# Sums of exponentials in three cross attentions: added and spread by one product with ones, inverted on all partitions in quarters

## The chip, the cores and the metric

The kernel runs on one core of one Trainium2 chip. TensorE does matrix products into eight PSUM banks of 128 x 512 float32; VectorE, ScalarE and GpSimd work on SBUF, the first two on PSUM as well; SyncE issues the loads. Each engine works through its own list of instructions in order, and they meet at semaphores. The metric is the device time of one execution in microseconds.

## The reference

Twelve sublayers of a small Perceiver: four rounds of cross attention, self attention and a feed-forward part over x, 8 sequences of 64 tokens of width 256. Three of the four cross attentions (L0, L1 and L3) read the 1601 rows of the context with 16 heads of 128. L1 and L3 have a mask (here all ones) and L0 normalises queries and keys by their root mean square. What matters here, from L3:

```python
scores = jnp.einsum('bhtd,bhsd->bhts', q, k) / scale
mask = vision_mask[:, None, None, :]
scores = jnp.where(mask, scores, -jnp.inf)
attn = jax.nn.softmax(scores, axis=-1)
attn = jnp.nan_to_num(attn, nan=0.0)
out = jnp.einsum('bhts,bhsd->bhtd', attn, v)
```

A softmax over 1601 keys needs the maximum and the sum of the exponentials of every query, and divides the output by that sum. The fourth cross attention (L2, the kind "dca") goes through the same function by branches of its own.

## The kernel before

`context_columns` (L301) does scores, softmax and values of one cross attention. Keys lie on the partitions, in 13 tiles of 128 (the last has 65 rows); the 512 columns are 8 heads x 64 queries of one sequence. A group g is one such half of a sequence's heads, so there are 16 groups of 13 tiles, and a step i is one tile. All engines walk the same list of steps; what one does at a step for an earlier tile is written as a delay.

- TensorE, at each step: the score product of tile i (L466) into one of three banks, then the value product of tile i - 18 (L483, `VAL` = 18), accumulated over a group. A score product waits until the maximum of the tile three steps back is taken (`maxed`; in the rms kind until it is kept).
- ScalarE: the exponential of tile i - 17 in place (L585), then the copy of the scores of tile i to SBUF (`probs`, a ring of 20 tiles; L604). In the rms kind the keys' scale is applied on the way, on ScalarE (L600) for four tiles of 13 and on VectorE (L677) for the others.
- VectorE: the subtraction of the maxima from tile i - 16 (the shift, L666), then the running maximum of tile i over the partitions' own rows (L689; L687 or L691 for the first tile, L693 in the kinds without mask).
- GpSimd: the sum of the exponentials, tile after tile, into `acc` (L763 copies the first, L766 adds the others).
- In the rms kind also two products of the key projection per step (L420), their squares (L539, ScalarE) and sums of squares (L620, VectorE); in every second group a mean square (L641), a root (L589) and its inverse (L646 to L650) on the way to the keys' scale.

Over the partitions, sums and maxima are taken through TensorE. For the maxima: four turns of `top` (L498) into bank 4 (`T_BANK`) at step 0 of the next group, a reduction along the columns (L711), and four products that spread the result over all partitions (L507). For the sums of group g the same path runs at steps counted in the later group whose tile i is then at hand:

- step 5: TensorE turns `acc` in four pieces of 128 x 128 (L517) into bank 4;
- step 6: VectorE reduces to 128 x 4 (L716), in the masked kind clamps at 1e-30 (L719), and inverts (L729 in L0, L1 and L3);
- step 7: TensorE spreads the four columns by four products with the identity (L528) into bank 4; a float32 product is two instructions, a turn is one;
- step 8: VectorE multiplies the kept values in `QT` by bank 4 (L741). ScalarE had copied them there at step 5 (L578).

The turn of the maxima, L498, comes right behind the value product of step 0. It waits until VectorE has taken the maximum of the group's last tile (tile 12), and until the multiplication two groups back has read bank 4. After the last score step only the pipeline's end runs, and then `heads_out` (L771) begins with L786.

Of the kernel before, what the change touches and what calls it, by code (L numbers as in the profile page):

```python
# [300 lines left out]
def context_columns(nc, M, A, kind, scale, W):  # L301
# [13 lines left out]
    T_BANK, X_BANK = 4, 6  # L315
    HALF = 2 * BANK
# [4 lines left out]
    with ExitStack() as ctx:  # L321
# [5 lines left out]
        if not dca:  # L327
            rows = sb("ctx_rows", [P, 2, NT, CDIM])
# [12 lines left out]
        with stage(nc, "first_in", "keys_in0", "keys_in1", "keys_in2", "rows_in0", "rows_in1", "ready", "scored", "by_act",  # L341
                   "by_dve", "maxed", "top_turned", "most_ready", "most_spread", "shifted", "exped", "valued", "summed",
                   "value_kept", "sum_turned", "sum_ready", "sum_clamped", "rest_ready", "rest_spread", "divided", "folded",
# [67 lines left out]
            def _(pe):  # L411
# [38 lines left out]
                for i in STEPS:  # L450
# [61 lines left out]
                    if g is not None:  # L512
                        pe.wait_ge(S["summed"], NT * (g + 1))
                        if g + 1 < NG:
                            pe.wait_ge(S["most_ready"], g + 2)
                        for b in range(4):
                            last = nc.tensor.transpose(M.bank[T_BANK][:, b * P:(b + 1) * P], acc[:, g % 2, b * P:(b + 1) * P],  # L517
                                                       M.ident[:, :])
                        last.then_inc(S["sum_turned"], 1)
                    g = due(i, NT + VAL + 2)  # L520
                    if g is not None:
                        pe.wait_ge(S["rest_ready"], g + 1)
                        for b in range(4):
                            if dca:
                                last = nc.tensor.matmul(M.bank[T_BANK][32 * b:32 * b + 32, 0:P], apart[:, g % 2, b, :],
                                                        M.ident[:, :], start=True, stop=True)
# [88 lines left out]
            def _(dve):  # L615
# [43 lines left out]
                for i in STEPS:  # L659
# [53 lines left out]
                    if g is not None:  # L713
                        z = rest[:, g % 2, :]
                        dve.wait_ge(S["sum_turned"], g + 1)
                        nc.vector.tensor_reduce(z, turned, AX.X, ALU.add).then_inc(S["sum_ready"], 1)  # L716
                        if kind == "mask":
                            dve.wait_ge(S["sum_ready"], g + 1)
                            nc.vector.tensor_scalar(z, z, 1e-30, None, ALU.max).then_inc(S["sum_clamped"], 1)  # L719
                            dve.wait_ge(S["sum_clamped"], g + 1)  # L720
                        else:
                            dve.wait_ge(S["sum_ready"], g + 1)
                        if dca:
                            step(nc.vector.reciprocal(z, z))
                            nc.vector.tensor_tensor(apart[:, g % 2, :, :], z.unsqueeze(2).broadcast_to([P, 4, 32]),
                                                    pair[:, :].unsqueeze(1).broadcast_to([P, 4, 32]),
                                                    ALU.mult).then_inc(S["rest_ready"], 1)
                        else:
                            nc.vector.reciprocal(z, z).then_inc(S["rest_ready"], 1)  # L729
                    g = due(i, NT + VAL + 3)  # L730
                    if g is not None:
                        dve.wait_ge(S["rest_spread"], g + 1)
                        dve.wait_ge(S["value_kept"], g + 1)
                        if dca:
                            x, o = part[:, g % 2, :], M.OT[:, g % U, g // U * SEQ:(g // U + 1) * SEQ]
                            step(nc.vector.tensor_tensor(x, x, M.bank[T_BANK][:, 0:P], ALU.mult))
                            step(nc.vector.tensor_tensor(o, o, x[:, 0:SEQ], ALU.add))
                            nc.vector.tensor_tensor(o, o, x[:, SEQ:P], ALU.add).then_inc(S["divided"], 1)
                        else:
                            x = M.QT[:, g // U, HG * (g % U):HG * (g % U + 1), :]  # L740
                            nc.vector.tensor_tensor(x, x, M.bank[T_BANK].rearrange("p (h q) -> p h q", h=HG),  # L741
                                                    ALU.mult).then_inc(S["divided"], 1)

            @block.gpsimd
            def _(pool):
# [8 lines left out]
                for i in STEPS:  # L754
                    if 0 <= i - VAL < NI:
# [1742 lines left out]
```

## Time and profile before

| | us |
|---|---|
| median of 3 runs | 3653.46 |
| lowest and highest | 3650.73, 3654.89 |
| profiled execution: its time | 3651.31 |
| profiled execution: span from first to last instruction | 3649.6 |
| TensorE busy | 3019.9 |
| VectorE busy | 2369.7 |
| ScalarE busy | 1677.3 |
| GpSimd busy | 1147.3 |

The profile is one execution taken by the hardware profiler. Its time has 1.7 us around the span. A row in order of time begins with the start in us from the span's start and the length; what stands in brackets at its end is how long the engine was idle before and what ended that. Several like instructions in a row are merged, with their count (x8); neighbours on an engine can overlap by a little, so the spacing of starts is the cost of an instruction in a full queue, and the length is what a waiting one sees. PE is TensorE, PEld its weight load, DVE VectorE, ACT ScalarE, POOL GpSimd. L0's groups run from about 200 to 915 us, L1's from 1350 to 1770, L3's from 2950 to 3370.

### The profile page before, as it was taken

The page shows a single profiled execution, that of the slowest core. Times are in us where ns is not written, and L with a number is a line of the kernel's source. Part 1 is how long each engine was busy: PE and PEld are TensorE (multiplying, and loading weights), DVE is VectorE, ACT ScalarE, POOL GpSimd, SP SyncE. Part 2 cuts the span into 40 slices and gives each one's busy share as a digit, 9 for nine tenths or more (in the row PEclk, how much of TensorE's full clock was granted, in tenths as well). Part 3 has the DMA queues.
Part 4 walks back from the last instruction along what each step waited for, and adds up shares of the span by engine and source line. Part 5 has one row for each costly group of instructions (what it writes and reads, how often), then busy time and mean ns, then how long its engine had stood idle before and what let it go on. Part 6 is the DMA issues. An engine that isn't in the chain of part 4 may idle for free. (4 is left out here: it accounts for less than half of the span.)

```text
span 3649.6 us, 35780 instructions
## 1 busy us (share of the span) xinstructions
PE 3019.9 (83%) x10841; PEld 1534.1 (42%) x10842; DVE 2369.7 (65%) x3813; ACT 1677.3 (46%) x3342; POOL 1147.3 (31%) x952
## 2 busy tenths in 40 slices
PE   7899999998898979999813378888845789999896
PEld 2344444443566634444501233333324434444563
DVE  4688888887275437777295557777854357776246
ACT  2455555555242226666311156666611146665241
POOL 0023333336000006666260035565710036666000
PEclk9999999999899989999856689999957899999998
DMA  1100000000420020110010100000010121100301
GB/s 61 75 0 19 19 19 19 19 10 0 111 71 1 0 95 28 37 37 10 13 51 8 37 18 10 19 10 1 1 37 6 41 75 37 37 28 1 107 1 41
DMA packets 73488, 110.58 MB, mean 30 GB/s; under 512 B 15792, under 2 KB 61776, under 8 KB 71888
## 3 DMA queue, kind: packets, MB, share of 16 engines
q1 hardware_dynamic: 73296, 108.29, 9.2%
q8 instruction: 88, 1.44, 0.2%
q14 instruction: 104, 0.85, 0.1%
HBM read 107.23 MB, written 1.05 MB: 30 GB/s over the span
## 5 line engine op out<-in xcount | busy, mean ns | idle before, releaser
L766 POOL TENSOR_TENSOR acc<-acc,probs 128x512 f32<-128x512 f32 (+2 forms) x768 | 981.2, 1278 | 797.1 <-ACT probs L585 773.6
L466 PE MATMUL psum<-QT,ctxT 128*128 128x512 f32 (+1 forms) x1248 | 638.2, 597 | 29.2 <-DMA ctxT<-in_ctx_T 26.6
L483 PE MATMUL psum<-probs,ctx_rows 128*128 128x512 f32 (+1 forms) x1248 | 633.4, 594 | 17.0 <-ACT probs L585 7.3
L666 DVE TENSOR_TENSOR probs<-probs,psum 128x512 f32<-128x512 f32 (+2 forms) x832 | 558.4, 675 | 27.6 <-PE psum L507 27.6
L604 ACT COPY probs<-psum 128x512 f32<-128x512 f32 (+2 forms) x624 | 362.9, 582 | 286.1 <-PE psum L466 282.6
L420 PE MATMUL psum<-wk_sb,ctxT 128*128 128x512 f32 (+1 forms) x832 | 391.1, 598 | 28.8 <-DMA ctxT<-in_ctx_T 17.1
L689 DVE SCALAR_TENSOR_TENSOR top<-psum,hidden,top 128x512 f32<-128x512 f32 (+1 forms) x384 | 287.5, 749 | 155.2 <-ACT probs L604 153.1
L763 POOL COPY acc<-probs 128x512 f32<-128x512 f32 x64 | 45.4, 709 | 1056.5 <-ACT probs L585 1056.5
L483 PEld LDWEIGHTS psum<-probs,ctx_rows 128*128 128x128 f32 (+1 forms) x1248 | 234.0, 190 | 319.9 <-issue 278.6
L539 ACT ACTIVATE ksq<-psum 128x1024 f32<-128x1024 f32 (+1 forms) x208 | 212.5, 1022 | 314.5 <-PE psum L420 311.3
L466 PEld LDWEIGHTS psum<-QT,ctxT 128*128 128x128 f32 (+1 forms) x1248 | 218.9, 188 | 253.3 <-issue 207.4
L585 ACT ACTIVATE probs<-probs,hidden 128x512 f32<-128x512 f32 (+1 forms) x416 | 299.3, 724 | 56.0 <-DVE probs L666 55.8
L585 ACT ACTIVATE probs<-probs 128x512 f32<-128x512 f32 (+2 forms) x416 | 259.8, 627 | 62.0 <-DVE probs L666 61.3
L620 DVE TENSOR_REDUCE key_var<-ksq 128x8 f32<-128x1024 f32 (+1 forms) x208 | 251.7, 1211 | 34.3 <-ACT ksq L539 34.3
L420 PEld LDWEIGHTS psum<-wk_sb,ctxT 128*128 128x128 f32 (+1 forms) x832 | 153.5, 187 | 240.1 <-issue 182.4
L466 PE MATMUL psum<-QT,keysT 128*128 128x512 f32 (+1 forms) x416 | 229.0, 634 | 1.2 <-ACT keysT L563 1.2
L693 DVE TENSOR_TENSOR top<-probs,top 128x512 f32<-128x512 f32 x192 | 145.9, 760 | 108.9 <-ACT probs L600 104.4
L693 DVE TENSOR_TENSOR top<-psum,top 128x512 f32<-128x512 f32 x192 | 132.0, 688 | 101.7 <-ACT probs L604 101.2
L751 POOL TENSOR_TENSOR kn<-kn,rk 128x256 f32<-128x256 f32 (+1 forms) x104 | 62.6, 624 | 281.7 <-DVE rk L650 281.7
L434 PE MATMUL psum<-wkv,ctxT 128*128 128x512 f32 (+1 forms) x208 | 116.7, 650 | 10.8 <-DMA ctxT<-in_ctx_T 7.5
L600 ACT ACTIVATE probs<-psum,rk 128x64 f32<-128x64 f32 x512 | 111.3, 335 | 5.1 <-PE psum L466 5.1
L479 PEld LDWEIGHTS psum<-probs,vals 128*32 128x32 f32 (+1 forms) x1664 | 34.0, 111 | 178.2 <-ACT probs L585 79.5
(423 smaller groups left out, 4064.5 us busy)
## 6 DMA issues: line engine op xcount, KB each, us to landing
ctx_rows<-in_ctx_rows SPq DMA_DIRECT2D x24, 832.0 KB, 4.5
ctxT<-in_ctx_T SPq DMA_DIRECT2D x24, 800.5 KB, 5.4
ctxT<-in_ctx_T SPq DMA_DIRECT2D x8, 792.5 KB, 4.5
wq_sb<-in_L_xattn_Wq SPq DMA_DIRECT2D x3, 2048.0 KB, 7.8
wo_sb<-in_L_xattn_Wo SPq DMA_DIRECT2D x3, 2048.0 KB, 9.9
wd<-in_L_ffn_wd SPq DMA_DIRECT2D x1, 3072.0 KB, 11.5
w_q<-in_L_attn_w_aq SPq DMA_DIRECT2D x8, 256.0 KB, 3.3
w_o<-in_L_attn_w_ao SPq DMA_DIRECT2D x1, 2048.0 KB, 10.1
```

The lines of the kernel that those rows point to most:

```text
L420: last = nc.tensor.matmul(M.bank[bank + j][0:hi - lo, :], ctxT[:, s % KEYS, lo:hi], wk[:, half * HALF + j * BANK:half * HALF + (j + 1) * B ...
L434: nc.tensor.matmul(M.bank[X_BANK + t % 2][0:hi - lo, :], ctxT[:, s % KEYS, lo:hi], wkv[:, :], start=True, stop=True).then_inc(S["projected ...
L466: nc.tensor.matmul(M.bank[i % BANKS][0:m, :], key, M.QT[:, s, HG * (g % U):HG * (g % U + 1), :], start=True, stop=True).then_inc(S["scored ...
L483: last = nc.tensor.matmul(M.bank[V_BANKS[g % len(V_BANKS)]], rows[0:m, s % 2, t, :], probs[0:m, j % RING, :], start=t == 0, stop=t == NT - 1)
L539: nc.scalar.square(ksq[0:hi - lo, v % 2, :], flat[0:hi - lo, bank * BANK:bank * BANK + HALF]).then_inc(S["squared"], 1)
L585: nc.scalar.activation(x, x, ACT.Exp, bias=bias, scale=scale).then_inc(S["exped"], 1)
L604: nc.scalar.copy(probs[0:m, i % RING, :], M.bank[i % BANKS][0:m, :]).then_inc(S["by_act"], 1)
L620: nc.vector.tensor_reduce(var[0:hi - lo, s % SLOTS, t, HG * half:HG * (half + 1)], ksq[0:hi - lo, v % 2, :].rearrange("p (h d) -> p h d", ...
L666: nc.vector.tensor_tensor(x, x, M.bank[M_BANKS[g % len(M_BANKS)]][0:m, :], ALU.subtract).then_inc(S["shifted"], 1)
L689: last = nc.vector.scalar_tensor_tensor(x, bank, hidden[0:m, s, t:t + 1], x, ALU.add, ALU.max)
L693: last = nc.vector.tensor_tensor(x, kept if norm else bank, x, ALU.max)
L766: nc.gpsimd.tensor_tensor(a, a, x, ALU.add).then_inc(S["summed"], 1)
```

## The change

In the kinds "rms" and "mask" the path of the sums is replaced. At step 5 TensorE does one product of a 128 x 128 matrix of ones with `acc` (128 x 512) into bank 4, so that each partition holds the sum of every column. VectorE inverts bank 4 in four quarters of 128 columns into a new SBUF tensor `inverse`, one quarter at each of the steps 6 to 9, behind the maximum of the step. At step 10 it multiplies `QT` by `inverse`. The turns of `acc`, the reduction, the clamp, the small reciprocal and the four spreads are gone there; so that no sum is zero, GpSimd adds 1e-32 to the first tile of a group in the masked kind where it copied it. The turn of the maxima now waits for the four quarters of two groups back in place of the multiplication. The kind "dca" keeps its instructions; the branches are only written in another order. The core of the diff:

```diff
+    QUARTERS = 4
+            inverse = sb("inverse", [P, N])
...
                         if g >= 2:
-                            pe.wait_ge(S["divided"], g - 1)
+                            if dca:
+                                pe.wait_ge(S["divided"], g - 1)
+                            else:
+                                pe.wait_ge(S["inverted"], QUARTERS * (g - 1))
...
                         if g + 1 < NG:
                             pe.wait_ge(S["most_ready"], g + 2)
-                        for b in range(4):
-                            last = nc.tensor.transpose(M.bank[T_BANK][:, b * P:(b + 1) * P], acc[:, g % 2, b * P:(b + 1) * P],
-                                                       M.ident[:, :])
+                        if not dca:
+                            last = nc.tensor.matmul(M.bank[T_BANK], M.ones[:, :], acc[:, g % 2, :], start=True, stop=True)
...
                     g = due(i, NT + VAL + 2)
-                    if g is not None:
+                    if g is not None and dca:
...
-                            else:
-                                last = nc.tensor.matmul(M.bank[T_BANK][:, b * P:(b + 1) * P],
-                                                        rest[:, g % 2, b:b + 1].broadcast_to([P, P]), M.ident[:, :],
-                                                        start=True, stop=True)
...
-                        if kind == "mask":
-                            dve.wait_ge(S["sum_ready"], g + 1)
-                            nc.vector.tensor_scalar(z, z, 1e-30, None, ALU.max).then_inc(S["sum_clamped"], 1)
-                            dve.wait_ge(S["sum_clamped"], g + 1)
...
-                            nc.vector.reciprocal(z, z).then_inc(S["rest_ready"], 1)
+                    for n in range(QUARTERS):
+                        g = due(i, NT + VAL + 1 + n) if not dca else None
+                        if g is not None:
+                            dve.wait_ge(S["sum_turned"], g + 1)
+                            these = slice(n * N // QUARTERS, (n + 1) * N // QUARTERS)
+                            nc.vector.reciprocal(inverse[:, these], M.bank[T_BANK][:, these]).then_inc(S["inverted"], 1)
+                    g = due(i, NT + VAL + 1 + QUARTERS) if not dca else None
+                    if g is not None:
+                        dve.wait_ge(S["inverted"], QUARTERS * (g + 1))
+                        dve.wait_ge(S["value_kept"], g + 1)
+                        x = M.QT[:, g // U, HG * (g % U):HG * (g % U + 1), :]
+                        nc.vector.tensor_tensor(x, x, inverse[:, :].rearrange("p (h q) -> p h q", h=HG), ALU.mult).then_inc(S["divided"], 1)
...
-                            x = M.QT[:, g // U, HG * (g % U):HG * (g % U + 1), :]
-                            nc.vector.tensor_tensor(x, x, M.bank[T_BANK].rearrange("p (h q) -> p h q", h=HG),
-                                                    ALU.mult).then_inc(S["divided"], 1)
...
-                            nc.gpsimd.tensor_copy(a, x).then_inc(S["summed"], 1)
+                            if kind == "mask":
+                                nc.gpsimd.tensor_scalar(a, x, 1e-32, None, ALU.add).then_inc(S["summed"], 1)
+                            else:
+                                nc.gpsimd.tensor_copy(a, x).then_inc(S["summed"], 1)
```

## Rows read from the trace of the kernel before

**Rows 1.** Busy time by stretch: us, then PE, PEld, DVE, ACT, POOL, clock, DMA.

```profile
250.00:300.00 50.00, 49.27 (x133) 22.88 (x132) 41.91 (x55) 28.26 (x61) 16.34 (x13) 1.00 0.00 1
850.00:900.00 50.00, 45.07 (x138) 20.73 (x137) 41.54 (x68) 26.64 (x74) 35.86 (x27) 1.00 0.00 1
1500.00:1550.00 50.00, 49.39 (x151) 23.97 (x150) 38.52 (x62) 32.33 (x54) 30.89 (x26) 1.00 0.10 34
```

**Rows 2.** Order of time, TensorE, L1: start, length, engine, line, out<-in, idle before.

```profile
1512.33 0.60 PE L498 MATMUL psum<-ident,top 128*128 128x128 f32 x4
...
1520.53 1.02 PE L466 MATMUL psum<-QT,ctxT 128*128 128x512 f32 x2
...
1522.25 0.60 PE L517 MATMUL psum<-ident,acc 128*128 128x128 f32 x4
1522.68 1.02 PE L466 MATMUL psum<-QT,ctxT 128*128 128x512 f32 x2
...
1525.26 1.02 PE L483 MATMUL psum<-probs,ctx_rows 128*128 128x512 f32 x2
1526.59 1.16 PE L528 MATMUL psum<-ident,rest 128*128 128x128 f32 x8 [0.30 <-DVE rest L729]
1527.58 1.02 PE L466 MATMUL psum<-QT,ctxT 128*128 128x512 f32 x2
...
1537.88 0.60 PE L498 MATMUL psum<-ident,top 128*128 128x128 f32 x4
```

**Rows 3.** Order of time, VectorE, the same group of L1.

```profile
1524.36 0.75 DVE L689 SCALAR_TENSOR_TENSOR top<-psum,hidden,top 128x512 f32<-128x512 f32 x1 [0.57 <-ACT probs L604]
1525.03 0.68 DVE L716 TENSOR_REDUCE rest<-psum 128x4 f32<-128x512 f32 x1
1525.74 0.58 DVE L719 TENSOR_SCALAR rest<-rest 128x4 f32<-128x4 f32 x1
...
1526.45 0.66 DVE L666 TENSOR_TENSOR probs<-probs,psum 128x512 f32<-128x512 f32 x1
...
1530.52 0.68 DVE L666 TENSOR_TENSOR probs<-probs,psum 128x512 f32<-128x512 f32 x1
1531.12 0.74 DVE L689 SCALAR_TENSOR_TENSOR top<-psum,hidden,top 128x512 f32<-128x512 f32 x1
1531.78 0.68 DVE L666 TENSOR_TENSOR probs<-probs,psum 128x512 f32<-128x512 f32 x1
```

**Rows 4.** Groups by line and shape: the reciprocals; busy us, mean ns, idle before.

```profile
L646 DVE RECIPROCAL rk<-rk 128x208 f32<-128x208 f32 x16 | 23.1, 1443 | 1.0 <-ACT rk L589 1.0
...
L291 DVE RECIPROCAL q_root<-q_root 128x512 f32<-128x512 f32 x4 | 13.4, 3343 | 0.0
...
L729 DVE RECIPROCAL rest<-rest 128x4 f32<-128x4 f32 x48 | 8.5, 178 | 1.6
```

**Rows 5.** Order of time, all engines, L0: VectorE and GpSimd on SBUF.

```profile
512.43 1.26 POOL L766 TENSOR_TENSOR acc<-acc,probs 128x512 f32<-128x512 f32 x1 [2.70 <-ACT probs L585]
...
513.10 1.14 DVE L693 TENSOR_TENSOR top<-probs,top 128x512 f32<-128x512 f32 x1
```

**Rows 6.** Order of time, all engines: the end of L1's head groups.

```profile
1747.79 16.79 POOL L766 TENSOR_TENSOR acc<-acc,probs 128x512 f32<-128x512 f32 x12 [0.39 <-ACT probs L585]
...
1764.63 1.12 PE L517 MATMUL psum<-ident,acc 128*128 128x128 f32 x4 [5.41 <-POOL acc L766]
...
1769.06 0.69 DVE L741 TENSOR_TENSOR QT<-QT,psum 128x512 f32<-128x512 f32 x1 [2.17 <-PE psum L528]
```

**Rows 7.** Order of time, TensorE, L0.

```profile
517.91 1.05 PE L528 MATMUL psum<-ident,rest 128*128 128x128 f32 x8
...
528.78 1.98 PE L420 MATMUL psum<-wk_sb,ctxT 128*128 128x512 f32 x4 [1.23 <-ACT ksq L539]
...
859.39 0.66 PE L498 MATMUL psum<-ident,top 128*128 128x128 f32 x4 [1.00 <-DVE top L693]
```

**Rows 8.** The page's groups by line: ScalarE's exponential in the masked kind.

```profile
L585 ACT ACTIVATE probs<-probs,hidden 128x512 f32<-128x512 f32 (+1 forms) x416 | 299.3, 724 | 56.0 <-DVE probs L666 55.8
```

More of the change, by code:

```diff
@@ L515, in _ @@
                             pe.wait_ge(S["most_ready"], g + 2)
[L516 to L518 removed]
+                        if not dca:
+                            last = nc.tensor.matmul(M.bank[T_BANK], M.ones[:, :], acc[:, g % 2, :], start=True, stop=True)
+                        else:
+                            for b in range(4):
+                                last = nc.tensor.transpose(M.bank[T_BANK][:, b * P:(b + 1) * P], acc[:, g % 2, b * P:(b + 1) * P],
+                                                           M.ident[:, :])
                         last.then_inc(S["sum_turned"], 1)
                     g = due(i, NT + VAL + 2)
[L521 removed]
+                    if g is not None and dca:
                         pe.wait_ge(S["rest_ready"], g + 1)
                         for b in range(4):
[L524 to L530 removed]
+                            last = nc.tensor.matmul(M.bank[T_BANK][32 * b:32 * b + 32, 0:P], apart[:, g % 2, b, :],
+                                                    M.ident[:, :], start=True, stop=True)
                         last.then_inc(S["rest_spread"], 1)
@@ L712, in _ @@
                     g = due(i, NT + VAL + 1)
-                    if g is not None:
+                    if g is not None and dca:
                         z = rest[:, g % 2, :]
@@ L716, in _ @@
                         nc.vector.tensor_reduce(z, turned, AX.X, ALU.add).then_inc(S["sum_ready"], 1)
-                        if kind == "mask":
-                            dve.wait_ge(S["sum_ready"], g + 1)
-                            nc.vector.tensor_scalar(z, z, 1e-30, None, ALU.max).then_inc(S["sum_clamped"], 1)
-                            dve.wait_ge(S["sum_clamped"], g + 1)
[L721 to L728, printed above, removed]
-                            nc.vector.reciprocal(z, z).then_inc(S["rest_ready"], 1)
+                        dve.wait_ge(S["sum_ready"], g + 1)
@@ new lines, in _ @@
+                        step(nc.vector.reciprocal(z, z))
+                        nc.vector.tensor_tensor(apart[:, g % 2, :, :], z.unsqueeze(2).broadcast_to([P, 4, 32]),
+                                                pair[:, :].unsqueeze(1).broadcast_to([P, 4, 32]),
+                                                ALU.mult).then_inc(S["rest_ready"], 1)
+                    for n in range(QUARTERS):
[4 more added lines that the diff above has]
+                            nc.vector.reciprocal(inverse[:, these], M.bank[T_BANK][:, these]).then_inc(S["inverted"], 1)
@@ L730, in _ @@
+                    g = due(i, NT + VAL + 1 + QUARTERS) if not dca else None
[4 more added lines that the diff above has]
+                        nc.vector.tensor_tensor(x, x, inverse[:, :].rearrange("p (h q) -> p h q", h=HG), ALU.mult).then_inc(S["divided"], 1)
                     g = due(i, NT + VAL + 3)
-                    if g is not None:
+                    if g is not None and dca:
@@ L732, in _ @@
                         dve.wait_ge(S["rest_spread"], g + 1)
                         dve.wait_ge(S["value_kept"], g + 1)
[L734 to L739, printed above, removed]
-                            x = M.QT[:, g // U, HG * (g % U):HG * (g % U + 1), :]
-                            nc.vector.tensor_tensor(x, x, M.bank[T_BANK].rearrange("p (h q) -> p h q", h=HG),
-                                                    ALU.mult).then_inc(S["divided"], 1)
+                        x, o = part[:, g % 2, :], M.OT[:, g % U, g // U * SEQ:(g // U + 1) * SEQ]
@@ L744, in _ @@
+                        step(nc.vector.tensor_tensor(x, x, M.bank[T_BANK][:, 0:P], ALU.mult))
+                        step(nc.vector.tensor_tensor(o, o, x[:, 0:SEQ], ALU.add))
+                        nc.vector.tensor_tensor(o, o, x[:, SEQ:P], ALU.add).then_inc(S["divided"], 1)
             @block.gpsimd
@@ L762, in _ @@
                                 pool.wait_ge(S["sum_turned"], g - 1)
-                            nc.gpsimd.tensor_copy(a, x).then_inc(S["summed"], 1)
+                            if kind == "mask":
+                                nc.gpsimd.tensor_scalar(a, x, 1e-32, None, ALU.add).then_inc(S["summed"], 1)
+                            else:
+                                nc.gpsimd.tensor_copy(a, x).then_inc(S["summed"], 1)
                         else:
```

2 lines of the change are left out of this document (1 added, 1 removed).

## The prediction

> **What bounds the kernel now.** I read the busy time by stage first, because the change touches three stages of twelve. In the two masked cross attentions (L1 and L3) TensorE is busy 49.39 of 50 us and VectorE 38.52; in the rms one (L0) 49.27 and 41.91; at the end of L0, where no more keys are projected, 45.07 and 41.54 [rows 1]. So TensorE's order of work sets the time, and VectorE follows with a reserve of some 11 us per 50 in the masked stages. That average hides when the reserve is there, so I read one head group (13 tiles, one step each) in order of time, on TensorE and on VectorE. From one turn of the maxima to the next is 25.55 us (1512.33 to 1537.88), and a plain step of one score product and one value product is 1.72 (1520.53 to 1522.25), two units of 0.86 [rows 2].
>
> **Removed from TensorE, masked stages.** The four turns of the sums, L517, take 0.43 (1522.25 to 1522.68). The four spreads, L528: the value product at 1525.26 would have let the next product start at 1526.12; it starts at 1527.58, so the spreads with their wait for the reciprocal cost 1.46 [rows 2]. Together 1.89 per group.
>
> **Added to TensorE.** One float32 product of 128x512 with ones. It is of the same form as the score and value products: 0.86; at most 1.02 if none of its latency were covered [rows 2]. It is 512 columns in two passes, just what the spreads had, so only the turns and the wait are saved: 1.89 - 0.86 = 1.03 per group, if nothing else becomes late.
>
> **Removed from VectorE.** The sum over turned columns, the clamp and the small reciprocal: 1525.03 to 1526.45, 1.42 in one step [rows 3]. The clamp is 0.58 of it although it handles four columns.
>
> **Added to VectorE.** Four reciprocals of 128 columns, from PSUM. The trace has the reciprocal at 4, 208 and 512 columns: 178, 1443 and 3343 ns [rows 4], a straight line of 6.2 ns per column, so 178 + 124 x 6.2 = 947 ns for 128. Neighbours overlap by some 0.08 us (L666 takes 0.68 and the next starts 0.60 later [rows 3]), so a quarter costs 0.87. No row shows it from PSUM; bounds are 0.80, if more of its head overlaps, and 0.95 without overlap. L666 reads PSUM at no visible extra, so I take 0.87. Four are 3.48, a net 2.06 more per group. The multiplication L741 stays, moved from step 8 to step 10, and reads two SBUF tensors; I take 0.60, as L666's spacing.
>
> The Trainium skill, "VectorE: DVE Perf Modes", section "First, the fixed hardware budget", says that the reciprocal is an iterative division with a repeat count of 8. Taken as eight passes at the 0.96 GHz that the page gives, 128 columns would be an estimated 1.07 us plus a head, dearer than the line above; by it the third rival below would be the forecast. The rows' 6.2 ns per column would be six passes at that clock, so the trace does not agree, and for SBUF operands the measurement decides.
>
> **Where VectorE gets late.** A plain VectorE step is the shift, 0.60, and the maximum, 0.66 (1530.52, 1531.12, 1531.78), 1.26 against TensorE's 1.72 [rows 3]. A quarter adds 0.87: 2.13, so VectorE falls behind by 0.41 in each of the steps that hold one. Measured from the start of step 6's score product: its maximum comes 1.68 later, as now (1522.68 to 1524.36 [rows 2, 3]). Then the quarter at 2.34, next shift 3.21, quarters at 4.47, 6.60 and 8.73, shift of step 10 at 9.60, multiplication at 10.86, shift of step 11 at 11.46, of step 12 at 12.72, its maximum at 13.32, done at 14.07 (0.75). TensorE reaches the next turn of the maxima eight steps after step 6: 8 x 1.717 = 13.74. That turn, L498, waits for just this maximum. With 0.15 for the hand-over (L528 starts 0.14 after VectorE has gone on from the reciprocal that it waits for, 1526.45 and 1526.59 [rows 2, 3]) it starts at 14.22, 0.48 late. The score products need the maximum three steps back, and those ends come earlier. A value product needs the exponential of the shift two steps before; the latest is step 0's, late by about 0.1, which lies inside the 0.48. Now the turn comes 15.20 after step 6's score (1522.68 to 1537.88 [rows 2]). New period: 25.55 + 0.43 (product 0.86 for turns 0.43) - (15.20 - 14.22) = 25.00. So 0.55 gained per group, about half of 1.03; the new wait is L498 for L689. The steps from 0 to 5 have no quarter, and there VectorE catches up.
>
> **Sum, one masked stage.** 13 of 16 groups have a full group behind them: 13 x 0.55 = 7.2. In the next the maximum, already what its turn waits for, comes 0.3 later: -0.3. The last group's sums are on the path: from L517 to the end of L741 now 1764.63 to 1769.75, 5.12 [rows 6]. There TensorE has idled and four turns take 1.12 instead of 0.60, so the ones product is 1.02 x 1.12 / 0.60 = 1.9; then 3 x 0.87 + 0.95 + 0.69 and two hand-overs of 0.05: 6.2, so -1.1. GpSimd adds 1e-32 in place of a copy, which costs at most a two-tensor addition, 1.26 [rows 5]; 0.39 of idle lies behind it in the last group [rows 6], and GpSimd has 19 of 50 us free before that [rows 1]: 0 to -0.8, I take -0.2. Together 7.2 - 0.3 - 1.1 - 0.2 = 5.6; two stages, 11.2.
>
> **The rms stage.** The spreads wait for nothing here (busy 1.05 against 1.16 [rows 7, 2]): about 0.89, so 0.43 + 0.89 - 0.86 = 0.46 gained in 11 groups, 5.1. In every second group the squares wait 1.23 for a root that VectorE's mean square releases [rows 7]; by then VectorE has done three quarters (2.6) in place of reduction, reciprocal and multiplication (1.4); most of the 1.2 falls into idle time, and I take a quarter of it, 5 x 0.3 = 1.5 lost. In the last three groups, without keys, the turn of the maxima already waits 1.00 for VectorE [rows 7]; 3.48 - 0.81 = 2.67 is added (0.81 is the 1.42 without the clamp and its hand-over) there per group, bounds 0 and 2.67. VectorE is idle 8.46 of 50 us there [rows 1], so I take 0.9 each, 2.6. Tail as above without clamp: 1.3. 5.1 - 1.5 - 2.6 - 1.3 is -0.3: nothing, between +5 and -7. The fourth cross attention (L2) keeps its code.
>
> Profiled execution: 3651.3 - 11.2 = 3640.1. Its time is 2.15 below the median of the runs, 3653.46, so the forecast is 3642.
>
> **Rivals.** *VectorE keeps up.* If the lag is half a microsecond smaller than I add up, L498 waits for nothing and the full 1.03 counts: 2 x (13 x 1.03 - 1.6) = 23.6, with some 3 from rms: 3626. For it: 11 us of reserve per 50 [rows 1]. Against: the reserve is not in steps 6 to 12. 0.16.
>
> *The multiplication meets GpSimd.* A VectorE operation on two SBUF tensors that starts while GpSimd adds takes 1.14 (513.10) where the addition began at 512.43 and ended at 513.69 [rows 5]: it ran only after it. L741 read PSUM; the new one does not. By my walk it starts 1.26 after step 10's shift, and GpSimd's next addition not before 1.40 (shift 0.68 [rows 3], exponential 0.72 [rows 8]), so it comes first. If the order is the other way it waits for a whole addition, 1.26 more: the gain of 0.55 becomes a loss of 0.71 in 26 groups: 3653.5 + 18 + 3 = 3675. Slower than before from a wait of 0.55 on; half an addition gives 3656. 0.15. The Trainium skill, "SBUF — State Buffer", section "Who interferes with whom", has this as a rule: two SBUF inputs contend with a GpSimd read, and whoever issues first blocks the other.
>
> *The reciprocal from PSUM is dearer.* If PSUM costs the head of 178 ns once more and nothing overlaps, a quarter is 1.12 [rows 4]; four add 1.0 to the lag and make the gain a loss of 0.45: 3653.5 + 12 + 3 = 3668. It turns at 1.01 per quarter. 0.11.
>
> *The moved work is hidden on both sides:* the spreads' wait returns in full as L498's wait, within 4 us of now. 0.10. Forecast: 0.48.
>
> **Numbers.** What a measurement of this kernel can tell from no change is about 0.2%, 7.3 us. Forecast 3642, its own range 3632 to 3651 (quarters between 0.80 and 0.95 move 26 groups by -7 to +8, rms by 5). Over all cases 3622 to 3671 leaves out some 2 in 10. Faster: 0.16 of the first rival and 0.41 of the forecast, 0.57. Same: 0.07 of the forecast, 0.10, and 0.06 of the port rival, 0.23. Slower: 0.20.
>
> **What would show it.** Right: 48 groups with one L517-like product of two passes, no spreads; reciprocals of 0.94 to 0.96, 192 of them; a masked period near 25.0; L498 waiting some 0.5 for L689. Wrong: multiplications over 1 us with GpSimd busy ahead of them; reciprocals over 1 us; a period of 24.5 without wait at L498; rms groups longer than now because the root comes later.

## The result, and the profile after

The changed kernel takes 3646.93 us (median of 20 runs, 3641.99 to 3655.57) against 3653.76 for the kernel before (20 runs): a ratio of 0.9981, 95% interval [0.9975, 0.9987], or 6.8 us less. The forecast was 3642, a gain of 11.5. The gain is real and lies just under the bound of 0.2% that the prediction took for what can be told from no change.

The sum over the stages hides two large terms of opposite sign. From the first score product of a stage to its first output product (L786 before, L791 after):

| stage | before | after | difference | forecast |
|---|---|---|---|---|
| L0, rms | 757.9 | 766.4 | +8.5 | about 0 |
| L1, masked | 424.2 | 416.8 | -7.5 | -5.6 |
| L3, masked | 424.0 | 416.6 | -7.5 | -5.6 |

Together -6.4. The two profiled spans differ by only 1.6 (3649.6 and 3648.0), since stretches whose code is unchanged took about 5 more in this execution; from the first output product of L1 to the first score of L3 the profiles of this study, all with the same code there, lie between 1171.8 and 1177.9. So times of stages and periods of groups are compared below, and medians for the whole.

Busy time by stretch after (us, then PE, PEld, DVE, ACT, POOL, clock, DMA), which answers to [rows 1]:

```profile
250.00:300.00 50.00, 49.27 (x124) 22.26 (x124) 44.52 (x58) 28.35 (x61) 16.34 (x13) 1.00 0.00 1
850.00:900.00 50.00, 42.06 (x107) 17.83 (x106) 45.34 (x67) 23.98 (x71) 32.20 (x23) 0.97 0.00 1
1500.00:1550.00 50.00, 49.91 (x135) 22.93 (x134) 42.90 (x65) 33.03 (x56) 34.06 (x27) 1.00 0.10 34
```

VectorE is 2.6 to 4.4 us busier per 50 in all three. In the masked stretch TensorE is busier too, 49.91, so it has lost idle time; at the end of L0 it is less busy, 42.06, so it waits more.

The page's groups after (busy us, mean ns | idle before):

```profile
L766 POOL TENSOR_SCALAR acc<-probs 128x512 f32<-128x512 f32 x32 | 47.6, 1488 | 798.6 <-ACT probs L588 798.6
...
L730 DVE RECIPROCAL inverse<-psum 128x128 f32<-128x128 f32 x192 | 180.9, 946 | 30.8 <-PE psum L522 30.8
```

The 192 quarters take 946 ns, where [rows 4] gave 947 by a straight line. GpSimd's new scalar addition takes 1.49 us.

One group of L1 on TensorE after, in order of time, to set beside [rows 2]:

```profile
1493.82 0.66 PE L503 MATMUL psum<-ident,top 128*128 128x128 f32 x4
...
1503.79 1.02 PE L522 MATMUL psum<-acc,ones 128*128 128x512 f32 x2
1504.65 1.02 PE L468 MATMUL psum<-QT,ctxT 128*128 128x512 f32 x2
...
1517.52 1.02 PE L485 MATMUL psum<-probs,ctx_rows 128*128 128x512 f32 x2
1518.59 0.66 PE L503 MATMUL psum<-ident,top 128*128 128x128 f32 x4
```

The ones product holds TensorE for 0.86 (1503.79 to 1504.65). The period from turn to turn is 24.77, where it was 25.55. The turn could have started at 1517.52 + 0.86 = 1518.38 and starts at 1518.59: it waits 0.21.

The same group on VectorE, beside [rows 3]:

```profile
1506.33 0.75 DVE L692 SCALAR_TENSOR_TENSOR top<-psum,hidden,top 128x512 f32<-128x512 f32 x1 [0.99 <-ACT probs L607]
1506.99 0.95 DVE L730 RECIPROCAL inverse<-psum 128x128 f32<-128x128 f32 x1
1507.86 0.63 DVE L669 TENSOR_TENSOR probs<-probs,psum 128x512 f32<-128x512 f32 x1
1508.40 0.74 DVE L692 SCALAR_TENSOR_TENSOR top<-psum,hidden,top 128x512 f32<-128x512 f32 x1
...
1515.25 0.69 DVE L736 TENSOR_TENSOR QT<-QT,inverse 128x512 f32<-128x512 f32 x1
1515.85 0.69 DVE L669 TENSOR_TENSOR probs<-probs,psum 128x512 f32<-128x512 f32 x1
...
1517.79 0.75 DVE L692 SCALAR_TENSOR_TENSOR top<-psum,hidden,top 65x512 f32<-65x512 f32 x1
```

From 1506.33 on VectorE has no idle time until the maximum of the group's last tile, 1517.79, which the turn waits for. A step with a quarter lasts 2.07 (1506.33 to 1508.40), not 2.13.

The end of L1's head groups, all engines, beside [rows 6]:

```profile
1747.25 1.49 POOL L766 TENSOR_SCALAR acc<-probs 128x512 f32<-128x512 f32 x1
1748.89 17.04 POOL L771 TENSOR_TENSOR acc<-acc,probs 128x512 f32<-128x512 f32 x12
1765.99 2.08 PE L522 MATMUL psum<-acc,ones 128*128 128x512 f32 x2 [5.07 <-POOL acc L771]
1768.10 3.39 DVE L730 RECIPROCAL inverse<-psum 128x128 f32<-128x128 f32 x4 [10.16 <-PE psum L522]
1771.53 0.69 DVE L736 TENSOR_TENSOR QT<-QT,inverse 128x512 f32<-128x512 f32 x1
```

From the ones product to the end of the multiplication: 6.23, where turns, reduction, spreads and multiplication took 5.12.

### The profile page after: what moved, and what is told of

Read it like the earlier page. It is cut to its first block and busy times, and to the rows that moved or that the text cites. A ratio compares the mean times of both kernels' runs of the same rounds, so it can differ in the third digit from the quotient of the medians.

```text
span 3648.0 us, 34885 instructions
## 1 busy us (share of the span) xinstructions
PE 3012.5 (83%) x10362; PEld 1496.4 (41%) x10362; DVE 2465.1 (68%) x3877; ACT 1672.6 (46%) x3342; POOL 1184.5 (32%) x952
## 5 line engine op out<-in xcount | busy, mean ns | idle before, releaser
L422 PE MATMUL psum<-wk_sb,ctxT 128*128 128x512 f32 (+1 forms) x832 | 393.8, 602 | 32.7 <-DMA ctxT<-in_ctx_T 17.2
L468 PEld LDWEIGHTS psum<-QT,ctxT 128*128 128x128 f32 (+1 forms) x1248 | 227.2, 189 | 295.7 <-issue 246.1
L766 POOL TENSOR_SCALAR acc<-probs 128x512 f32<-128x512 f32 x32 | 47.6, 1488 | 798.6 <-ACT probs L588 798.6
L422 PEld LDWEIGHTS psum<-wk_sb,ctxT 128*128 128x128 f32 (+1 forms) x832 | 154.0, 188 | 244.6 <-issue 179.6
L730 DVE RECIPROCAL inverse<-psum 128x128 f32<-128x128 f32 x192 | 180.9, 946 | 30.8 <-PE psum L522 30.8
L768 POOL COPY acc<-probs 128x512 f32<-128x512 f32 x32 | 25.9, 810 | 264.4 <-ACT probs L588 264.4
```

What stands on the lines that cost most here:

```text
L422: last = nc.tensor.matmul(M.bank[bank + j][0:hi - lo, :], ctxT[:, s % KEYS, lo:hi], wk[:, half * HALF + j * BANK:half * HALF + (j + 1) * B ...
L468: nc.tensor.matmul(M.bank[i % BANKS][0:m, :], key, M.QT[:, s, HG * (g % U):HG * (g % U + 1), :], start=True, stop=True).then_inc(S["scored ...
L730: nc.vector.reciprocal(inverse[:, these], M.bank[T_BANK][:, these]).then_inc(S["inverted"], 1)
```

## Why L0 lost: the root, and the clock behind it

In five groups of L0 the squares wait for a root [rows 7]. VectorE before, in the group from which [rows 7] has the wait; these rows did not stand ahead of the prediction:

```profile
521.64 0.69 DVE L693 TENSOR_TENSOR top<-probs,top 128x512 f32<-128x512 f32 x1 [1.80 <-ACT probs L600]
522.25 1.21 DVE L620 TENSOR_REDUCE key_var<-ksq 65x8 f32<-65x1024 f32 x1
523.38 0.67 DVE L741 TENSOR_TENSOR QT<-QT,psum 128x512 f32<-128x512 f32 x1
523.97 0.68 DVE L666 TENSOR_TENSOR probs<-probs,psum 128x512 f32<-128x512 f32 x1
...
527.14 0.27 DVE L641 TENSOR_SCALAR key_var<-key_var 128x208 f32<-128x208 f32 x1
```

And after, all engines:

```profile
519.10 0.94 DVE L730 RECIPROCAL inverse<-psum 128x128 f32<-128x128 f32 x1
...
521.23 0.69 DVE L696 TENSOR_TENSOR top<-probs,top 128x512 f32<-128x512 f32 x1 [0.64 <-ACT probs L603]
...
522.96 0.94 DVE L730 RECIPROCAL inverse<-psum 128x128 f32<-128x128 f32 x1
523.83 0.62 DVE L669 TENSOR_TENSOR probs<-probs,psum 128x512 f32<-128x512 f32 x1
...
526.93 0.27 DVE L644 TENSOR_SCALAR key_var<-key_var 128x208 f32<-128x208 f32 x1
...
528.57 3.37 PE L422 MATMUL psum<-wk_sb,ctxT 128*128 128x512 f32 x4 [1.98 <-ACT ksq L542]
```

The quarter of step 7 (519.10) falls into the time in which VectorE waited for ScalarE's scaled copy: 1.80 of idle becomes 0.64. Nothing covers the quarter of step 8 (522.96), which stands where the multiplication of 0.67 (523.38) stood: from there to the mean square VectorE does not idle. Measured from the end of that wait, the mean square comes 5.70 later where it came 5.50 later. What TensorE saved does not shorten such a group, because its squares waited for the root before too: counted from the group's turn of the maxima (491.09 before, 490.60 after) they start 37.97 us in, where they started 37.69. So the wait grows from 1.23 to 1.98, and the group gets 0.33 longer instead of 0.47 shorter.

Behind that wait the clock falls in some groups. Two stretches after, in the columns of [rows 1]; the granted clock is the number behind POOL's count:

```profile
525.00:528.50 3.50, 1.59 (x4) 0.38 (x2) 3.43 (x6) 1.27 (x2) 0.00 (x0) 1.00 0.00 0
528.90:532.30 3.40, 3.40 (x5) 1.35 (x4) 3.37 (x4) 1.87 (x3) 1.26 (x1) 0.52 0.00 0
```

It is at its upper level, 2.4 GHz, through the wait, and at the lower, 1.2 GHz, for 3.4 us after it, so L422 takes 3.37 instead of 1.98. Two of the five groups have this and last 51.79 instead of 50.15; before, none had.

At the end of L0, without keys, the multiplication meets GpSimd:

```profile
859.34 1.70 POOL L771 TENSOR_TENSOR acc<-acc,probs 128x512 f32<-128x512 f32 x1 [1.03 <-ACT probs L588]
859.83 1.76 DVE L736 TENSOR_TENSOR QT<-QT,inverse 128x512 f32<-128x512 f32 x1
```

It begins 0.49 after the addition and ends 0.55 after it: 1.76 instead of 0.68.

## The experiments

Each is an edit of the changed kernel; "masked" is L1 and L3. The stages are timed as in the table above, the whole against the kernel before.

| kernel | L0 | L1 | L3 | whole (median) | ratio to before, interval |
|---|---|---|---|---|---|
| changed kernel | 766.4 | 416.8 | 416.6 | 3646.93 | 0.9981 [0.9975, 0.9987] |
| mask_only | 759.4 | 416.5 | 416.7 | 3639.41 | 0.9955 [0.9942, 0.9967] |
| rms_only | 766.7 | 424.6 | 424.3 | 3664.54 | 1.0025 [1.0016, 1.0035] |
| rms_spaced | 768.1 | 416.7 | 416.7 | 3651.80 | 0.9990 [0.9981, 0.9998] |
| rms_free8 | 759.1 | 416.8 | 416.7 | 3644.77 | 0.9974 [0.9963, 0.9984] |
| mask_late_mult | 766.5 | 413.9 | 413.7 | 3641.74 | 0.9961 [0.9948, 0.9973] |
| mask_fifth | 766.7 | 428.0 | 428.1 | 3670.24 | 1.0045 [1.0030, 1.0060] |
| mult_first | 766.6 | 426.6 | 426.5 | 3667.26 | 1.0033 [1.0021, 1.0046] |
| inverse_in_bank | 763.8 | 418.8 | 418.8 | 3646.45 | 0.9980 [0.9970, 0.9989] |
| plain_copy | 766.7 | 413.5 | 415.7 | 3644.8 (one run) | |
| mask_late_rms_old | 757.8 | 412.3 | 413.6 | 3636.13 | 0.9951 [0.9936, 0.9966] |
| combined | 754.6 | 413.7 | 413.8 | 3629.87 | 0.9931 [0.9917, 0.9944] |

The kernel before, measured beside them, had medians from 3653.46 to 3655.29, so two kernels are best compared by their ratios. Two differences between the stages have nothing to do with the edits. In plain_copy and mask_late_rms_old L1 took 14.3 us ahead of its first turn of the maxima, in the other profiles 15.6 to 16.0: there the granted clock was back at 2.4 GHz 2.9 us after L1's first score, in the changed kernel 6.1. And the end of L0, from its last turn to the first output product, took 30.0 in mask_only, where the code of L0 is the old one and the kernel before took 28.7: mask_only had 3.4 us at 1.2 GHz from 889.83 on.

**One stage kind at a time.** mask_only and rms_only make the change in one kind and keep turns, small reciprocal and spreads in the other (the lines are those of mask_only):

```diff
+    new = kind in ('mask',)
...
-                        if not dca:
+                        if new:
                             last = nc.tensor.matmul(M.bank[T_BANK], M.ones[:, :], acc[:, g % 2, :], start=True, stop=True)
```

> The changed kernel with the old path of the sums put back in L0, so the new path stands in L1 and L3 alone. Theory: the masked stages carry the whole gain (from first score to the first product of the head outputs 416.8 us each against 424.2 before) and L0 gives 8.5 us away. Then L0 takes 757.9 us again, the masked stages keep 416.8, and the time is about 14.9 us below before: some 3639 us. Rival: L0 is neutral, as the prediction had it, and what is missing is spread over the program; then the time stays near that of the changed kernel, 3647 us.

> The complement: the new path in L0 alone, the old one in L1 and L3. Theory: slower than before by some 8.5 us, about 3662 us, with the waits of the squares for the root at 1.98 us in every second group of L0 and stretches of TensorE's clock at half. Rival (L0 neutral): 3654 us, and a half clock in L0 only by chance of one execution.

Measured: 0.45%, 16 us, gained by the masked stages alone, and 0.25%, 9 us, lost by L0 alone. This is shown: the change is a good one in two stages and a bad one in the third.

**What makes the root late.** The first theory was that three quarters ahead of the mean square are too many. rms_spaced takes one of them away: L0's quarters at steps 6, 8, 11 and 12, its multiplication at step 2 of the next group.

```diff
+    Q_AT = {'mask': (1, 2, 3, 4), 'rms': (1, 3, 6, 7), 'dca': (1, 2, 3, 4)}[kind]
+    DIV_AT = {'mask': 5, 'rms': 10, 'dca': 5}[kind]
...
-            inverse = sb("inverse", [P, N])
+            inverse = sb("inverse", [P, 2, N])
...
-                        g = due(i, NT + VAL + 1 + n) if not dca else None
+                        g = due(i, NT + VAL + Q_AT[n]) if not dca else None
```

> The changed kernel, but in L0 the quarters stand at steps 6, 8, 11 and 12 instead of 6 to 9, and the multiplication at step 2 of the next group instead of step 10 (the inverse has two buffers for it). So only two quarters lie ahead of the mean square, 1.74 us in place of the old 1.4. Theory (the quarters make the root late, the longer idle lets the clock fall): wait for the root back to 1.2 to 1.5 us, no half clock in the middle groups, L0 some 6 us shorter than in the changed kernel (760 us from first score to head outputs), total about 3641 us. Rival (VectorE has too much to do in L0 wherever it stands): L0 stays at 766 us, total 3647 us.

Measured: the wait did not move, and L0 got longer.

```profile
531.00 1.98 PE L424 MATMUL psum<-wk_sb,ctxT 128*128 128x512 f32 x4 [1.99 <-ACT ksq L544]
```

So the count is not what matters, and that theory fell. The rows of VectorE above suggested the next one: only the quarter of step 8 lies uncovered. rms_free8 leaves step 8 free; its quarters are at steps 6 and 7, ahead of the mean square in step 9, and at 9 and 11 behind it, and its multiplication stands at step 2 of the next group, as in rms_spaced:

```diff
+    Q_AT = {'mask': (1, 2, 3, 4), 'rms': (1, 2, 4, 6), 'dca': (1, 2, 3, 4)}[kind]
```

> L0's quarters at steps 6, 7, 9 and 11 of a group, its multiplication at step 2 of the next one (inverse in two buffers); masked stages as in the changed kernel. Theory (only what VectorE does in the step ahead of the mean square, step 8, makes the root late; quarters at 6 and 7 fall into VectorE's wait for ScalarE): the mean square comes at about 35.5 after the group's start instead of 36.33, the root wait of the odd groups is 1.1 to 1.2 instead of 1.98, odd groups 49.3 instead of 50.15, no half clock in the middle groups, L0 from first score to first output product about 759 instead of 766, the whole 3639. Rival (the root is late by the step-7 square and by TensorE's own saving, not by a quarter at step 8): root wait 1.98 and odd groups 50.15 as before, the whole 3646.

```profile
521.15 0.69 DVE L698 TENSOR_TENSOR top<-probs,top 128x512 f32<-128x512 f32 x1 [0.64 <-ACT probs L605]
...
522.89 0.67 DVE L671 TENSOR_TENSOR probs<-probs,psum 128x512 f32<-128x512 f32 x1
...
526.05 0.27 DVE L646 TENSOR_SCALAR key_var<-key_var 128x208 f32<-128x208 f32 x1
...
527.69 1.98 PE L424 MATMUL psum<-wk_sb,ctxT 128*128 128x512 f32 x4 [1.17 <-ACT ksq L544]
```

The quarter of step 7 stands, with the same 0.64 of idle behind it; behind the sums of squares the shift follows at once (522.89). The mean square comes 4.90 after that wait's end instead of 5.70, and the projection waits 1.17. The five groups last 49.29 and L0 759.1, as expected; the groups between them last 48.09 instead of 47.83. The whole came out at 3644.77, 2 us below the changed kernel where 8 were expected. The two intervals overlap, and the stage, 7.3 shorter, is the sharper measure; where the other 5 us went is not shown. In the profiled executions the time outside the three stages lies between 2041 and 2050 us, whatever the kernel, and rms_free8's is the longest. Against each other rms_spaced and rms_free8 (both with two quarters ahead of the mean square) show that the step decides, and not the number.

**The clock.** No run was made for it alone, but the runs sort themselves. In the eight profiles in which these squares wait 1.98 to 2.03 the clock fell to 1.2 GHz behind 15 of 40 such waits; in the five in which they wait 1.17 to 1.24 (before, mask_only, rms_free8, mask_late_rms_old, combined) behind none of 25. In the same place of rms_free8:

```profile
527.70:531.00 3.30, 3.30 (x8) 1.62 (x9) 3.27 (x5) 3.16 (x4) 1.27 (x1) 1.00 0.00 0
```

Why some of the longer waits are followed by it and others are not stays open. The length of the wait alone does not decide: at the end of L0 in the kernel before, a value product waited 3.12 us (824.16) and the clock stayed at 2.4 GHz.

**Whether the masked stages have any reserve.** mask_fifth adds a fifth quarter, into a tensor that nobody reads, at step 9:

```diff
-    QUARTERS = 4
+    QUARTERS = 5 if kind == "mask" else 4
...
+                        g = due(i, NT + VAL + 1 + min(n, 3)) if not dca else None
...
+                            these = slice(min(n, 3) * P, (min(n, 3) + 1) * P)
+                            nc.vector.reciprocal(inverse[:, these] if n < 4 else spare[:, :], M.bank[T_BANK][:, these]).then_inc(S["inverted"], 1)
```

> A fifth reciprocal of 128 columns into a spare tensor at step 9 of the masked groups; its result is not used. Theory (VectorE's lag through steps 6 to 10 reaches the turn of the maxima with nothing to spare, so a further quarter of 0.87 lies wholly on the path): period 25.6 instead of 24.78, the whole 26 x 0.86 = 22 more, 3669. Rival (VectorE's reserve of 11 us per 50 takes it in): period 24.8, the whole 3647 to 3650.

```profile
1524.65 0.66 PE L503 MATMUL psum<-ident,top 128*128 128x128 f32 x4
...
1550.24 0.66 PE L503 MATMUL psum<-ident,top 128*128 128x128 f32 x4
```

Period 25.59: 0.81 more per group, nearly the whole of a quarter, and 23 us in all. The 7 us per 50 that VectorE is idle there cover almost none of it. mask_late_mult takes VectorE's work out of these steps instead: the multiplication moves to step 2 of the next group (inverse in two buffers).

```diff
+    DIV_AT = {'mask': 10, 'rms': 5, 'dca': 5}[kind]
```

> The changed kernel, but in L1 and L3 the multiplication stands at step 2 of the next group instead of step 10 (two buffers of the inverse). Theory: the turn of the maxima waits only because VectorE has four quarters and the multiplication between step 6 and step 12; with 0.6 us of that moved behind the turn the wait of 0.21 us goes, the period of a masked group falls from 24.78 to 24.57 us, where TensorE's own work sets it, and the time by 26 x 0.21 = 5.5 us, to about 3641 us. Rival (the multiplication is hidden, the wait comes from the exponentials): period 24.78 as now, 3647 us.

```profile
1517.71 0.60 PE L505 MATMUL psum<-ident,top 128*128 128x128 f32 x4
...
1542.22 0.60 PE L505 MATMUL psum<-ident,top 128*128 128x128 f32 x4
```

Period 24.51: 0.26 less. 25.55 - 1.03 = 24.52 is what the prediction gave for a VectorE that keeps up, so with the multiplication gone from step 10 all that TensorE saved counts in the period. The stage gets 2.9 shorter, and not 13 x 0.26 = 3.4, since its last two groups together take 0.5 longer.

**The rival with GpSimd's port.** mult_first puts the masked multiplication first in step 10, ahead of the shift, where an addition runs on GpSimd:

```diff
                 for i in STEPS:
+                    g = due(i, NT + VAL + 1 + QUARTERS) if kind == "mask" else None
+                    if g is not None:
...
                     if 0 <= i - SUB < NI:
```

> In the masked stages the multiplication stands first in step 10, ahead of the shift, so that it starts 0.6 after the addition of step 9 on GpSimd began instead of 0.26 before the next. Theory (a VectorE operation on two SBUF tensors waits for the GpSimd addition that runs): the multiplication takes 1.3 instead of 0.68, the delay lies on the path to the turn of the maxima, period 25.45 instead of 24.78, the whole 26 x 0.67 = 17 more, 3664: slower than the kernel before. Rival (the masked stages have no such contention, or it is taken in): multiplication 0.68, period 24.8, the whole 3647.

```profile
1517.09 1.27 POOL L777 TENSOR_TENSOR acc<-acc,probs 128x512 f32<-128x512 f32 x1 [0.79 <-ACT probs L588]
...
1517.81 1.10 DVE L668 TENSOR_TENSOR QT<-QT,inverse 128x512 f32<-128x512 f32 x1
...
1520.31 1.13 PE L485 MATMUL psum<-probs,ctx_rows 128*128 128x512 f32 x2 [0.70 <-ACT probs L588]
```

It ends 0.55 after the addition's end, as in L0; period 25.48, 20 us more, slower than before. The multiplication took 1.10 and not the 1.3 expected, 0.41 more than in the changed kernel, and the delay does not lie where the theory had it: the turn of the maxima no longer waits, but a value product waits 0.70 for the exponential of the shift behind the multiplication. So some 0.3 of the 0.70 per group comes from putting the multiplication ahead of the shift at all; no run separates the two. The rival's mechanism is real all the same, and its point is the order. In the changed kernel the multiplication starts 0.26 ahead of the addition (1515.25 above):

```profile
1515.51 1.55 POOL L771 TENSOR_TENSOR acc<-acc,probs 128x512 f32<-128x512 f32 x1 [0.79 <-ACT probs L588]
```

There it takes 0.68 to 0.69 in all 32 masked groups, and it is the addition that gets longer, 1.55 instead of 1.27. The Trainium skill, "SBUF — State Buffer", section "Who interferes with whom", has the rule that whoever issues first blocks the other; the two orders here agree with it.

inverse_in_bank takes one of the two SBUF operands away. The reciprocals are written in place in bank 4, the multiplication reads PSUM, and the turn of the maxima waits for the multiplication:

```diff
-                            nc.vector.reciprocal(inverse[:, these], M.bank[T_BANK][:, these]).then_inc(S["inverted"], 1)
+                            nc.vector.reciprocal(M.bank[T_BANK][:, these], M.bank[T_BANK][:, these]).then_inc(S["inverted"], 1)
```

> The reciprocals are written in place, in PSUM, and the multiplication reads PSUM instead of the SBUF tensor; the turn of the maxima waits for the multiplication. Theory (the multiplications of 1.07 and 1.76 in L0 wait for GpSimd because both operands lie in SBUF): all 48 multiplications take 0.68, the last two groups of L0 are about 1 each shorter, the whole 3644. Rival (they are long for another reason): the same long multiplications in L0, the whole 3647. In the masked stages the turn waits for the multiplication of step 10, 1.3 after the last quarter's step began, which is before the turn's own maximum: period 24.8 in both.

```profile
L727 DVE RECIPROCAL psum<-psum 128x128 f32<-128x128 f32 x192 | 182.1, 953 | 30.5 <-PE psum L519 30.5
...
L733 DVE TENSOR_TENSOR QT<-QT,psum 128x512 f32<-128x512 f32 x48 | 32.6, 678 | 0.1
```

All 48 multiplications take 0.68. The last two groups of L0 last 29.07 instead of 29.96, as expected, and L0 is 2.6 shorter. Not expected: the masked period is 24.95 instead of 24.78, since a step with a quarter lasts 2.11 when its result goes to PSUM. That gives the gain back, and the whole is that of the changed kernel; 3644 was expected.

**GpSimd's scalar addition.** plain_copy copies the first tile of a masked sum, as before:

```diff
-                                nc.gpsimd.tensor_scalar(a, x, 1e-32, None, ALU.add).then_inc(S["summed"], 1)
+                                nc.gpsimd.tensor_copy(a, x).then_inc(S["summed"], 1)
```

> GpSimd copies the first tile of a masked group's sums in place of adding 1e-32 to it; the guard against a sum of zero is left out. Theory (the scalar addition is on the path only in the last group of a stage): from the last turn of the maxima to the first output product 30.1 instead of 30.97 in both stages (1.49 - 0.61 = 0.88 less), periods 24.78 unchanged. Rival (the addition is hidden): 30.97.

```profile
3339.19 0.61 POOL L765 COPY acc<-probs 128x512 f32<-128x512 f32 x1
...
3357.08 2.08 PE L522 MATMUL psum<-acc,ones 128*128 128x512 f32 x2 [3.67 <-POOL acc L768]
```

From the last turn to the first output product of L3: 30.11 where the changed kernel has 30.96. In L1 it is 29.26: there the ones product ran at 2.4 GHz, in 1.12 instead of 2.08. The periods stay at 24.78. So the addition costs 0.85 at the end of a stage and nothing elsewhere, as far as one run shows.

**A version that beats both.** First the late multiplication in the masked stages with L0 left as it was before:

> Ones product, quarters and a multiplication at step 2 of the next group in the masked stages only; L0 keeps the turns, the small reciprocal and the spreads. Theory (the two effects add: masked-only 3639.4, and the late multiplication gave 5 more in the changed kernel): 3634, masked period 24.51, L0 759. Rival (part of the 5 came from elsewhere): 3639.

Measured 3636.13, 2 us more than expected; L0 757.8, period 24.51. Then also the new way in L0, with quarters at steps 6, 7, 9 and 11, but only in the groups that a group with keys follows:

```diff
+    Q_AT = {'mask': (1, 2, 3, 4), 'rms': (1, 2, 4, 6), 'dca': (1, 2, 3, 4)}[kind]
+    DIV_AT = 5 if kind == 'dca' else 10
+    CUT = {'mask': 16, 'rms': 12, 'dca': 0}[kind]
...
-                        if new:
+                        if g < CUT:
                             last = nc.tensor.matmul(M.bank[T_BANK], M.ones[:, :], acc[:, g % 2, :], start=True, stop=True)
```

> Masked stages: ones product, quarters, multiplication at step 2 of the next group. L0: the same with quarters at steps 6, 7, 9 and 11 in the 12 groups that a group with keys follows, and turns, small reciprocal and spreads in the last four. Theory (the gains are of separate stretches and add): L0 periods 48.09 and 49.29 with keys, 45.6 and 28.4 without, L0 from first score to first output product 754; the whole 3632. Rival (the gain of L0's middle groups is given back where the two ways meet): L0 758 or more, the whole 3636.

Measured 3629.87: 0.9931 [0.9917, 0.9944], 25 us under the kernel before and 17 under the changed one. L0 is 754.6, with periods of 48.09, 49.29 and 28.40; only the first group without keys, 46.39, is longer than the 45.6 expected, with 3.4 us at 1.2 GHz in it.

## Point by point: where the prediction was right and wrong

**Right: TensorE's terms.** The ones product costs 0.86, and 1.03 is saved where nothing else gets late (mask_late_mult).

**Right: the reciprocal.** 946 ns from PSUM against 947, spaced by 0.87 against 0.87. The rival of a dearer PSUM operand is out. The Trainium skill, "VectorE: DVE Perf Modes", section "First, the fixed hardware budget", with its repeat count of 8 would have made it an estimated 1.07 us plus a head; the measurement stands by the rows' straight line.

**Right in kind, too large: VectorE's lag.** The step with a quarter was taken as 2.13, and it is 2.06 to 2.07: the shift behind a quarter lets its successor start after 0.54 (1507.86 to 1508.40), not 0.60. Four of these make most of 0.28. The turn comes 13.94 after step 6's score (1504.65 to 1518.59) where 14.22 was added up, waits 0.21 and not 0.48, and the period is 24.78 and not 25.00. That it waits for the maximum of the last tile, with no reserve, was right (mask_fifth). In a masked stage 13 groups gain 10.2, not 7.2 (one 0.83, twelve 0.78).

**The next group:** 0.07 lost (24.70 to 24.77), not 0.3. **The masked end:** 6.23 against 5.12, the 1.1 that was added up. **GpSimd, wrong:** from the last turn to the product of the sums 23.15 became 24.42, 1.27 lost where -0.2 was taken and -0.8 was the bound. The step that failed took a two-tensor addition, 1.26, as the ceiling and set the 0.39 of idle time in [rows 6] against it; the scalar addition is dearer, 1.49, and no idle time is left behind it. 0.85 of the 1.27 is this (plain_copy). 0.25 more is that the twelve additions behind it take 17.04 instead of 16.79: one of them runs into the multiplication of the group before (1754.26) and takes 1.54 instead of 1.27. In inverse_in_bank, whose multiplication reads PSUM, the twelve take 16.78. So this is the same contention, on GpSimd's side, and the prediction had no price for it. The rest is a later start. With these, 10.2 - 0.1 - 1.1 - 1.3 = 7.7; the other 0.2 to 0.3 of a stage went ahead of its first turn (15.63 us from the first score in L1 before, 15.92 after), in work that the change does not touch.

**Wrong: the rms stage,** forecast at about 0 between +5 and -7, measured -8.5. Term by term: the six groups without a root wait gained 0.47 each, as predicted (0.46). The five others should have gained 0.46 and lost 0.3; they lost the whole saving to the wait and 0.33 on top, 4.0 in place of 1.5. Two steps failed. One is that 0.46 was booked for all 11 groups: in five of them TensorE already waited for the root, so that nothing TensorE saves shortens them, 2.3 in all. The other is "most of the 1.2 falls into idle time, and I take a quarter of it": it added up three quarters against idle time anywhere, where the only one that counts is the quarter in step 8, which stands between the sums of squares and the mean square without idle time. The clock behind two of these waits cost 1.64 each, 3.3; no step of the prediction had it. The groups without keys lost 1.45, 1.59 and 1.59, 4.6 in place of 2.6. The first has the clock at 0.51 of full speed for 6.8 us, but this is not shown to set its length: its turn waits 0.51 for VectorE's maximum all the same (834.84), and in rms_only and plain_copy, with 3.4 us at the lower clock, the group lasts 47.03 and 47.04 too. 0.9 of each of the last two is the multiplication that meets GpSimd (29.96 to 29.07 in inverse_in_bank), and the other 0.7 is left to VectorE's extra work, for which 0.9 had been taken; no run shows that part alone. The end lost 1.8, not 1.3; it has 3.4 us at 1.2 GHz behind the last turn (from 894.25), which the kernel before lacks and mask_only's old code has too, there with 1.4 more than before. So most of the 1.8 may be the clock. 5.1 - 4.0 - 3.3 - 4.6 - 1.8 = -8.6.

**The rivals.** VectorE did not keep up, but a kernel with the multiplication elsewhere does. The multiplication met GpSimd not in the masked stages, to which the rival's price of 18 us belonged, but in L0, which the prediction did not look at for it. Nothing was hidden on both sides. The forecast came within 5 us because the masked stages gave 3.7 more than it said and L0 took 8.5 that it had at nothing: the sign was right by the masked stages' reasoning, and the size is partly luck.

## What to carry to other kernels

Before work is moved to an engine that is busy 80 to 90%, find in each stage the step in which something on the critical path waits for that engine, and keep that step free: here the place of one reciprocal of 0.87 us decided most of 7 us. A change that is applied to several stages by one switch should be costed, and tried, stage by stage; two of three may pay for the third. Two SBUF operands on VectorE are cheap only while they start ahead of GpSimd's operation, and then it is GpSimd that loses time (1.55 instead of 1.27).

## What the runs showed of the hardware that was not expected

- GpSimd adds a constant to 128x512 float32 in 1.49 us, dearer than adding two such tensors (1.27); a copy takes 0.61 in the masked stages.
- VectorE's shift (128x512, one operand in PSUM) behind a reciprocal that wrote SBUF takes 0.63 and frees the engine after 0.54; behind one that wrote PSUM, or behind another elementwise operation, 0.67 and 0.59 to 0.60.
- A wait of 2 us on TensorE was followed by 3.4 us at 1.2 GHz in 15 of 40 cases; a wait of 1.2 us in the same place in none of 25.
